# Second attention of a fused two-layer network: another layout in DRAM of the split Q and K, and seven wider reads in place of twelve per portion

## The reference, cut to what matters

```
query = _layernorm(q @ Wq + bq, qn_scale, qn_bias)      # q: 512 tokens of the batch
key   = _layernorm(kv @ Wk + bk, kn_scale, kn_bias)     # kv: 512 context rows of the batch
value = _layernorm(kv @ Wv + bv, vn_scale, vn_bias)
scores = einsum('bhqd,bhkd->bhqk', query, key) / sqrt(16)     # 16 heads of 16 dimensions
probs = softmax(where(mask == 0, -1e9, scores))
out = einsum('bhqk,bhkd->bhqd', probs, value) @ Wo + bo
```

## Time and profile before

| what | value |
|---|---|
| median of 3 runs | 2315.28 us (2314.14 to 2317.16) |
| the profiled execution, its own time | 2316.27 us |
| its span in the trace | 2314.5 us |
| PE busy, share of the span | 1966.5 us, 85% |
| DVE busy | 1576.7 us, 68% |
| ACT busy | 1059.8 us, 46% |
| landing of a write of parts (512 KB) after its issue, median | 3.7 us |
| stretch from the first spread of batch 1 to the end of the attention | 686 to 1427 us |

### The profile page before, as it was taken

The page is one execution under the profiler, slowest core; times in us unless marked ns, Lnnn a source line. Parts: engine busy times, 40 slices in busy tenths (PEclk is TensorE's granted clock), DMA queues, the critical chain, the costliest instruction groups (busy, mean ns, idle before and its releaser), DMA issues. The chain is left out here.

```text
span 2314.5 us, 35806 instructions
## 1 busy us (share of the span) xinstructions
PE 1966.5 (85%) x12086; PEld 1392.0 (60%) x12086; DVE 1576.7 (68%) x3208; ACT 1059.8 (46%) x2039; POOL 919.2 (40%) x671
## 2 busy tenths in 40 slices
PE   5889888977598988989898989700999999999998
PEld 3566666664233433434343434600999999999998
DVE  7999999984565655656565753630777777777775
ACT  2233434433255554545555544210566566556554
POOL 6988888863433332323332200155222222222222
PEclk9899999988699999999999998555999999999999
DMA  7100000101624425151515310242566666666662
GB/s 286 43 10 8 10 10 10 35 1 34 109 74 67 84 53 102 32 105 33 97 60 78 76 21 1 73 173 91 189 222 227 211 225 222 224 224 216 228 216 68
DMA packets 146909, 245.79 MB, mean 106 GB/s; under 512 B 14235, under 2 KB 92143, under 8 KB 146802
## 3 DMA queue, kind: packets, MB, share of 16 engines
q1 hardware_dynamic: 135660, 218.93, 34.1%
q0 software_dynamic: 10624, 25.26, 2.9%
q10 hardware_dynamic: 518, 0.27, 0.0%
HBM read 201.96 MB, written 45.76 MB: 107 GB/s over the span
## 5 line engine op out<-in xcount | busy, mean ns | idle before, releaser
L1321 DVE CUSTOM_DVE_ANT_0 x_dump<-x_ps,x_bias_q 128x512 bf16<-128x512 f32 x512 | 353.3, 690 | 200.6 <-PE x_ps L1049 188.1
L1202 ACT ACTIVATE x_PT<-x_ps 128x512 f32<-128x512 f32 x512 | 290.1, 601 | 292.2 <-PE x_ps L1064 289.3
L1063 PE MATMUL x_ps<-x_bias_k,x_ident_b 128*128 128x512 bf16 x512 | 201.1, 393 | 66.5 <-DMA x_QS<-x_rows 66.4
L1852 ACT ACTIVATE e_silu<-m_ps 128x256 f32<-128x256 f32 x312 | 118.6, 380 | 231.9 <-PE m_ps L1789 231.9
L1756 POOL DMA_INDIRECT out_dram<-e_y,e_label x78 | 78.9, 1012 | 365.4 <-DVE e_y L1908 353.6
L1049 PE MATMUL x_ps<-x_KS,x_QS 96*128 96x512 bf16 x512 | 203.6, 399 | 12.0 <-DVE x_mx L1321 11.5
L1064 PE MATMUL x_ps<-x_QS,x_KS 98*128 98x512 bf16 x512 | 200.2, 391 | 0.0
L1891 DVE TENSOR_TENSOR e_gated<-e_silu,m_ps 128x256 f32<-128x256 f32 x312 | 120.7, 417 | 102.5 <-ACT e_silu L1852 98.0
L1789 PE MATMUL m_ps<-e_x_lo,m_hi 128*128 128x256 f32 x640 | 181.1, 283 | 1.5 <-DVE e_x_lo L1876 1.5
L1789 PE MATMUL m_ps<-e_x_hi,m_lo 128*128 128x256 f32 x640 | 181.0, 283 | 0.0
L1789 PE MATMUL m_ps<-e_x_hi,m_hi 128*128 128x256 f32 x640 | 180.7, 282 | 0.0
(11 more groups left out here) (291 smaller groups left out, 5517.4 us busy)
## 6 DMA issues: line engine op xcount, KB each, us to landing
m_raw<-in_L_ffn_w_dram SPq DMA_DIRECT2D x117, 1024.0 KB, 5.1
parts<-x_part SPq DMA_DIRECT2D x24, 512.0 KB, 3.7
expert_in<-a_blank SPq DMA_DIRECT2D x1, 10062.0 KB, 28.4
e_x<-expert_in SPq DMA_DIRECT2D x39, 258.0 KB, 5.8
x_QS<-parts SPq DMA_DIRECT2D x48, 192.0 KB, 8.8
x_KS<-parts SPq DMA_DIRECT2D x48, 192.0 KB, 12.1
next_mask_k<-in_maskT_dram SPq DMA_DIRECT2D x32, 256.0 KB, 2.7
next_mask_q<-in_mask_dram SPq DMA_DIRECT2D x29, 256.0 KB, 2.8
```

Of the source, the lines that this page charges most:

```text
L1063: pe.matmul(ps_st[e % 3], ident_b[:, :], bias_k[b % 2][:, kc, :], start=True, stop=False)
L1202: act.activation(PT[unit % 2][:, k, :], ps_st[e % 3], ACT.Exp, scale=DH ** -0.5).then_inc(exp_done, 1)
L1321: dve.tensor_tensor_reduce(out=dump[:, :], in0=ps_max[m % 2], in1=bias_q[b % 2][:, q, :], scale=1.0, scalar=NEG, op0=ALU.add, op1=ALU.max, ...
L1852: act.activation(silu[f % 2][:, :], ps_h[f % 4][:, 0:BLK], ACT.Silu).then_inc(silu_done, 1)
```

## The change: what it does

The DRAM tensor is laid out by stack (Q or K), part, head dimension, head pair, where it was by part, stack, head pair, head dimension. In this layout the 16 dimensions of part 0, of part 1 and of part 2 follow each other, so neighbouring slots that hold parts 0, 1 (and 2) are one transfer of 32 (or 48) partitions. The slots are put in an order that has such runs: Q has the parts 0 1 2 0 1 0, K has 0 1 0 1 0 2, which gives the same six products. A portion is then read in 7 transfers: for Q 48, 32 and 16 partitions, for K 32, 32, 16 and 16. For one partition, the head pairs of a portion are one contiguous stretch in DRAM (4 KB or 12 KB), where they were rows of 2 KB. To have the partitions come out in this order, the columns of Wq, Wk, their biases and the norm's scale and shift are reordered on loading (`by_pair`). All three parts must be in DRAM before the first read is issued, where the reads of part 0 waited for part 0 alone.

```
-Q_PARTS, K_PARTS = (0, 0, 1, 1, 0, 2), (0, 1, 0, 1, 2, 0)
+Q_RUNS = ((0, 3, 0), (3, 2, 0), (5, 1, 0))
+K_RUNS = ((0, 2, 0), (2, 2, 0), (4, 1, 0), (5, 1, 2))
+READS = len(Q_RUNS) + len(K_RUNS)

-                wait(sp, first_in, 16 * 2 * PARTS * (b - 1))
-                wait(sp, spread_in, 16 * 2 * PARTS * (b - 1))
-                sp.dma_start(kept[b % 2, part].rearrange("k e d n -> (e d) k n"),
+                wait(sp, first_in, 16 * READS * (b - 1))
+                wait(sp, spread_in, 16 * READS * (b - 1))
+                sp.dma_start(kept[b % 2, :, part].rearrange("k d e n -> (d e) k n"),

-            def spread_part(b, part, pairs, landed):
-
-                sp.wait_ge(*((rest_out, 32 * (b + 1)) if part else (hi_out, 16 * (b + 1))))
-                for k, (stack, order) in enumerate(((QS, Q_PARTS), (KS, K_PARTS))):
-                    for slot in range(PARTS):
-                        if order[slot] == part:
-                            to = stack[b % 2][slot * DH:(slot + 1) * DH, :, :].rearrange("d (e c) n -> d e (c n)", c=2)
-                            sp.dma_start(to[:, pairs, :], kept[b % 2, part, k].rearrange("e d n -> d e n")[:, pairs, :]).then_inc(landed, 16)
+            def spread(b, pairs, landed):
+
+                for k, (stack, runs) in enumerate(((QS, Q_RUNS), (KS, K_RUNS))):
+                    for slot, slots, part in runs:
+                        to = stack[b % 2][slot * DH:(slot + slots) * DH, :, :].rearrange("d (e c) n -> d e (c n)", c=2)
+                        of = kept[b % 2, k].rearrange("t d e n -> (t d) e n")[part * DH:(part + slots) * DH]
+                        sp.dma_start(to[:, pairs, :], of[:, pairs, :]).then_inc(landed, 16)

-                        for part in range(3):
-                            spread_part(b, part, slice(0, 2), first_in)
-                        for part in range(3):
-                            spread_part(b, part, slice(2, H // 2), spread_in)
+                        sp.wait_ge(hi_out, 16 * (b + 1))
+                        sp.wait_ge(rest_out, 32 * (b + 1))
+                        spread(b, slice(0, 2), first_in)
+                        spread(b, slice(2, H // 2), spread_in)

-    kept = nc.dram_tensor("parts", (2, 3, 2, H // 2, DH, 2 * SEQ), BF16, kind="Internal").ap()
+    kept = nc.dram_tensor("parts", (2, 2, 3, DH, H // 2, 2 * SEQ), BF16, kind="Internal").ap()
```

More of the change, by code:

```diff
@@ L971, in low_part @@
                 pool.wait_ge(mid_done, n + 1)
-                wait(pool, spread_in, 16 * 2 * PARTS * (n // TPB - 1))
+                wait(pool, spread_in, 16 * READS * (n // TPB - 1))
                 pool.tensor_tensor(part_at(n, 2), rest(n), part_at(n, 1), ALU.subtract).then_inc(lo_done, 1)
@@ L1044, in scores_for_maximum @@
                 if i == 0:
-                    pe.wait_ge(first_in, 16 * 2 * PARTS * (b + 1))
+                    pe.wait_ge(first_in, 16 * READS * (b + 1))
                 elif i == 16:
-                    pe.wait_ge(spread_in, 16 * 2 * PARTS * (b + 1))
+                    pe.wait_ge(spread_in, 16 * READS * (b + 1))
                 wait(pe, s1_used, m - 1)
@@ L1189, in high_part @@
                 act.wait_ge(full_done, n + 1)
-                wait(act, spread_in, 16 * 2 * PARTS * (n // TPB - 1))
+                wait(act, spread_in, 16 * READS * (n // TPB - 1))
                 act.activation(part_at(n, 0), full(n), ACT.Copy).then_inc(hi_done, 1)
@@ L1970, in by_dim, with by_pair @@
         return a.reshape(a.shape[:-1] + (H, DH)).swapaxes(-1, -2).reshape(a.shape)
+    def by_pair(a):
+        return a.reshape(a.shape[:-1] + (KC, H // KC, DH)).swapaxes(-1, -2).reshape(a.shape)
     def by_chunk(q, k):
-        return np.stack([q, k]).reshape(2 * KC, P).T
+        return np.stack([by_pair(q), by_pair(k)]).reshape(2 * KC, P).T
     def by_row(v):
@@ L1991 @@
             dram("w2T", get("L0_ffn_w2").T), dram("b2", get("L0_ffn_b2"))],
-           [*group("L1_xattn_", "Wq bq Wk bk Wv bv"),
+           [*(dram("L1_xattn_" + n, by_pair(get("L1_xattn_" + n))) for n in "Wq bq Wk bk".split()),
+            *group("L1_xattn_", "Wv bv"),
             *(dram(f"L1_xattn_qk_{n}", by_chunk(get(f"L1_xattn_qn_{n}"), get(f"L1_xattn_kn_{n}"))) for n in ("scale", "bias")),
```

## The result

| what | before | changed |
|---|---|---|
| median of 6 runs each | 2316.22 us (2314.14 to 2321.21) | 2248.31 us (2246.63 to 2250.47) |
| ratio, 95% interval | | 0.9706 (0.9694 to 0.9719) |
| the profiled execution: own time, span | 2316.27, 2314.5 us | 2248.76, 2247.0 us |
| its mean granted clock | 0.914 | 0.928 |

The change takes 67.9 us away; 71 were forecast, and 2248.3 lies in the range of 2238 to 2262. The two medians answer how much. Where it came from is read in the trace, in the same places as before.

What follows compares the result with a forecast made beforehand. PE was taken to bound the attention, waiting for rows of maxima held up by the spread. An excess of 74.7 us less 7 x 0.5 gives 71.2; 2316.27 less that is 2245.1, predicted as 2245, range 2238 to 2262.

Steps and rivals of the forecast that it cites:

- What bounds the kernel: Attention: PE bounds it, waiting 66.4 us for rows of maxima behind the spread (stack reads); excess 74.7 us over seven groups.
- Time of a spread: Stack reads on SP's queue: rate in proportion to partitions, up to 310 GB/s; a spread ends at 703.1, 9.7 us earlier.
- rival 2: Wide Q read no faster than two of 16 partitions, its outer thirds taking turns; 9 us left, 2251 us; chance 0.12.
- Loads behind it: Context tiles and masks on SP's queue go out after the spread, done at 705.1 and about 707.1.
- The rows: Rows of maxima land by 707.1 or 707.7, PE free at 707.81; wait near nothing, 0.5 us left for each group.
- With waits this short the clock holds: PE in the groups behind a spread: after waits of about 1 us its granted clock stays 1.00.
- The wait for all three parts: Ahead of the first read: costs nothing; in batch 0 that read moves from 588.09 to about 591.7, under 8 us cover.
- The writes and the reordered weights: Writes of parts to DRAM with changed spacing, and weights reordered on loading: both cost nothing at run time.
- rival 1: As forecast, the rows land within about 1 us of PE's need; 2239 to 2250 us; chance 0.70.
- Rival 3: Engines walk a wide stack read sixteen neighbouring partitions at a time; rate stays 114 GB/s, no change, 2316; chance 0.08.
- rival 5: Slower: reading 12 KB stretches 16 KB apart in DRAM runs below 114 GB/s; 2379 at 90 GB/s; chance 0.04.
- Rival 4: Half a cure: rows wait behind long packets, or 3 to 4 us waits stay and the clock drops; 2281; chance 0.06.

Runs made afterwards that it cites:

- e4_left_out: Kernel before; from batch 2 on the second portion reads one head pair of six, a sixth of the bytes in as many transfers; 2251.81 us, ratio 0.9732.
- e1_narrow: Changed kernel with each slot read by itself, 12 transfers of 16 partitions per portion, new layout kept; 2309.45 us, ratio 0.997.
- e2_short_rows: Changed kernel with the DRAM tensor padded so the 7 wide reads go in rows of 2 KB again; 2254.06 us, ratio 0.9727.
- e3_upper: Changed kernel with its runs in another order: the read of 48 goes to partitions 48 to 95, K reads move too; 2244.15 us, ratio 0.9686.
- e7_hold_all: Changed kernel with e3_upper's slots; SP holds the loads behind the spread, first mask included, until the rows land, except one context tile; 2240.8 us, ratio 0.9681.
- e8_rates: Copy-only kernel without the computation, reading 12 KB rows into partition ranges one transfer at a time; 576 KB took 4.6 us into 48-95, 6.0 into 0-47.
- e5_hold: Changed kernel; SP issues the loads that go out 1 to 2 us before the rows only once the rows have landed; 2245.27 us, ratio 0.9702.
- e9_rows_first: As e7_hold_all, with the wait for the third group's rows moved ahead of the writes of the middle and low part; 2247.55 us, ratio 0.97.
- a2_hold_again: The kernel of e7_hold_all run once more, beside a repeat of the changed kernel; 2239.11 us, ratio 0.9679.

## Why the prediction came out as it did

**What bounds the kernel** was right: PE bounds the stage, its wait was one for the rows, and the reads cost by what they hold up. e4_left_out takes the bytes away without touching anything else and the wait goes; the changed kernel does the same by rate.

**Time of a spread** is the term of the sum that was mis-sized. It was to fall by 9.7 us, from 26.0 to 16.3. The count of bytes seems to agree (from 687.3 to 703.7), but what the rows wait behind is the landing of the last read. The time from the first issue of a spread to that landing, as a mean of batches 1 to 7, stands here beside the sum of the seven stretches:

| kernel | spread, us | seven stretches, us |
|---|---|---|
| before | 28.7 | 220.0 |
| e1_narrow | 26.8 | 209.6 |
| e2_short_rows | 20.5 | 157.8 |
| changed | 20.2 | 156.0 |
| e3_upper | 19.0 | 151.0 |
| e7_hold_all | 18.8 | 146.9 |

It fell by 8.5 us, between the 9.7 of the forecast and the 7.6 of rival 2. The step that gave 9.7 is the rate in proportion to the partitions. A read into partitions 0 to 47 isn't at full pace (e8_rates), and with other places the spread is 1.2 us shorter (e3_upper). The other error is of opposite sign: rows of 12 KB are read somewhat faster than those of 2 KB (187 against 169 GB/s, 0.35 us for each spread). The sentence on source rows of 2 KB, "no different for a mask", took a load at 310 GB/s into 128 partitions as proof that row length costs nothing into 16 to 48, and e1_narrow and e2_short_rows show that it does.

**Loads behind it.** Priced as a queue behind the spread they came out shorter than forecast: four of them landed within 2.2 us of the last read in batch 1 and within 3.4 in the other batches (4.0 forecast), and the one mask of the last batch within 0.6 us (0.9 forecast). But they don't only stand behind the spread. Issued from 693.18 on, they run beside its last packets on the same DMA engines, and e5_hold and e7_hold_all show that this costs time. In the last batch the two together made PE lose 3.93 us and its clock where 0 to 1 us was forecast.

**The rows.** 0.5 us for each group was left, 3.5 in all; the seven stretches have 156.0 - 145.3 = 10.7 us. That is 7.2 too little. The total hides half of it by luck, since 3.7 us went the other way in the tail, which the change doesn't touch; so 2248.8 stands where the sum had 2245.1. The experiments take the 10.7 us apart, each by the sum of the seven stretches. Other places for the reads take it from 156.0 to 151.0, holding the loads of the last 2 us to 149.6, holding the mask too to 146.9. 1.6 us are left over the floor, nearly all in the last batch. So about half of the excess goes with the places of the reads, and most of the rest with the loads behind the spread. The waits of PE came to 17.1 us with a longest of 3.9, where about 10 were to be seen, all near 1.

**With waits this short the clock holds** was mostly right: six stretches of the changed kernel have a granted clock of 1.00. It isn't a rule, and before had the counterexample in a place that I had not read. A window of the kernel before, behind a wait of 1.94 us at 1002.58 ahead of a spread:

```profile
1003.00:1007.00 4.00, 4.00 (x14) 2.04 (x13) 1.44 (x5) 1.68 (x3) 0.00 (x0) 0.57 0.43 122
```

A wait of 2.10 us in the changed kernel cost no clock, and neither did those of 2.18 us in e1_narrow and 2.21 in e9_rows_first; those of 2.01 in e7_hold_all and 2.08 in e2_short_rows did. Of the waits for rows in these traces none of up to 1.81 us was followed by a lower clock, and all from 2.30 us on were. What decides between the two in the cases from 1.94 to 2.21 us is not shown.

**The wait for all three parts** cost nothing, as said: in batch 0 the first read is issued at 592.20 (591.7 forecast) and no wait of PE follows. **The writes and the reordered weights**: no trace of either.

**The rivals.** 2248.3 lies in rival 1's range of 2239 to 2250, but in the profiled execution it is there by the tail: the 10.7 us left are more than rival 1's 1.2 us for each group (8.4) and nearer to rival 2's 9. Rival 2 named a real mechanism and gave 2251, so the total alone would not have told them apart. It is e8_rates that shows the mechanism and e3_upper that prices the places, at 5.0 us of the 10.7. Rival 3 and rival 5 fall with the 187 GB/s. Rival 4's wait of 3 to 4 us with a dropped clock came true in one group of seven. Its figure of 2281 doesn't follow from its own terms: 2316.3 less 74.7 and 35 more is 2276.6.

**Left open.** Why 8 KB on ACT's queue have to wait until what SP issued earlier is nearly drained, rather than take turns with it, is shown as behaviour by four kernels and was not tried as a mechanism. The trace of the kernel before adds that the rows' packets do not even begin. They have a DMA queue of their own, q10, and for the rows issued at 704.62 it moves nothing from 704.7 to 714.8. Here is the queue of SP's transfers (q1) in that window, and then q10 from 714.8 to 715.2 (packets, MB, share of 16 engines):

```profile
q1 hardware_dynamic: 894, 1.24, 107.1%
...
q10 hardware_dynamic: 13, 0.01, 6.5%
```

The waits ahead of the spread, 0.5 to 1.8 us in a2_hold_again, have a known cause, but e9_rows_first only traded them for worse.

## What to carry to other kernels

When an engine waits for a small transfer, look at what was issued before it on other queues: here 60 us of waits for 8 KB were the price of 3 MB written 16 partitions at a time. Make the bulk wide and keep a transfer off partitions 32 apart below 64; then hold back loads that nobody needs yet until the small one has landed, which gave 9.5 us more for the order of slots and one wait. Price a backlog by when its last transfer lands, not by when a count of bytes is full, and read the group with the least work separately: its stall comes first.

## What the runs showed of the hardware

A transfer of 12 KB rows into 16 partitions alone takes 3.5 us and one of twice the bytes into 32 takes 3.9; 96 partitions with 1152 KB take 7.1, and all 128 with 1536 KB only 6.8. In the spread of batch 1 neither the width nor the size of a transfer changes its 0.42 to 0.46 us of issue on SP's queue. Two transfers of 4 KB on ACT's queue, issued at 704.62 into a backlog of SP's, began to move only 10.2 us later. And PE's clock fell to its lower level after a wait of 1.94 us in one place and stayed up after 2.21 us in another.
